# Two groups of query products instead of three, a stream shuffle for the rotary halves, and the rotary sums on POOL

## The reference

```python
q = _rms_norm(x @ w_qa, q_a_norm_w) @ w_qb          # 16 heads of 128 + 64
q_nope, q_rope = (q[..., :D_NOPE], q[..., D_NOPE:])
q_rope = q_rope * cos + rotate_half(q_rope) * sin   # (-x2, x1) on even and odd features
scores = einsum(q_full, k_full) * scale             # causal mask, softmax, times v
```

## Time and profile before

| | before |
|---|---|
| median of 3 runs | 1178.39 us (1176.42 to 1179.44) |
| the profiled execution | 1178.33 us, span 1176.4 us |
| mean granted TensorE clock | 0.985 |
| busy: PE, DVE, ACT, POOL | 1114.3, 818.9, 791.4, 699.2 us |
| three query matmuls, L1101 (32 pairs x 3 groups) | 96 groups |
| POOL `q_lo`, L904 | 64 times, 1341 ns mean |

### The profile page before, as it was taken

One profiled execution on the slowest core, in us unless ns is written; L12 is line 12 of the kernel. 1 busy time (PEld: TensorE's weight loads), 2 busy tenths in 40 slices (PEclk: granted clock), 3 DMA queues, 4 the chain that ended last, 5 costly groups with the idle time before them and its releaser, 6 DMA issues. The chain is left out here.

```text
span 1176.4 us, 27725 instructions
## 1 busy us (share of the span) xinstructions
PE 1114.3 (95%) x11356; PEld 930.9 (79%) x11356; DVE 818.9 (70%) x1825; ACT 791.4 (67%) x1104; POOL 699.2 (59%) x579
## 2 busy tenths in 40 slices
PE   5769999999999999999999999999999788999997
PEld 4747788888888888888888888888887687989886
DVE  3778767676767777676767778677676566675776
ACT  3737777877778787778778787877877543333232
POOL 1436776877777677877676776868777662130000
PEclk9889999999999999999999999999999989999999
DMA  9430100010002000100100020010000050000000
GB/s 241 111 116 17 32 20 9 12 48 20 20 2 65 2 20 26 41 20 2 54 12 20 1 65 15 6 48 20 19 2 2 15 166 1 1 19 1 19 18 18
DMA packets 58126, 39.60 MB, mean 34 GB/s; under 512 B 8113, under 2 KB 57329, under 8 KB 57841
## 3 DMA queue, kind: packets, MB, share of 16 engines
q1 hardware_dynamic: 56608, 33.81, 10.3%
q10 hardware_dynamic: 1392, 4.03, 1.3%
HBM read 33.37 MB, written 4.46 MB: 32 GB/s over the span
## 5 line engine op out<-in xcount | busy, mean ns | idle before, releaser
L912 POOL TENSOR_TENSOR pt_lo<-pt 128x1024 f16<-128x1024 f32 x192 | 370.4, 1940 | 182.1 <-ACT pt L969 181.8
L1031 DVE TENSOR_REDUCE gates<-bank 128x1 f32<-128x512 f32 x384 | 261.6, 689 | 147.8 <-PE bank L1113 144.9
L960 ACT ACTIVATE pair<-shift 128x1024 f32<-128x1024 f32 x256 | 263.5, 1029 | 12.5 <-ACT pt L973 0.7
L969 ACT ACTIVATE pt<-pair 128x1024 f32<-128x1024 f32 x192 | 196.0, 1021 | 110.0 <-PE pair L1141 109.3
L1156 PEld LDWEIGHTS bank<-values,pt 128*128 128x128 bf16 x2176 | 196.8, 98 | 80.4 <-issue 52.5
L1156 PE MATMUL bank<-values,pt 128*128 128x65 f16 x2176 | 235.2, 195 | 6.2 <-DVE lat L1057 5.5
L1158 PE MATMUL bank<-values,pt 128*128 128x64 f16 x2176 | 231.8, 192 | 0.0
L1160 PE MATMUL bank<-values,pt_lo 128*128 128x65 f16 x2176 | 230.8, 194 | 0.0
L918 POOL TENSOR_TENSOR pt_lo<-pt 128x512 f16<-128x512 f32 (+3 forms) x256 | 178.3, 723 | 46.4 <-ACT pt L973 46.3
L1158 PEld LDWEIGHTS bank<-values,pt 128*128 128x128 bf16 x2176 | 202.0, 98 | 0.0
L1160 PEld LDWEIGHTS bank<-values,pt_lo 128*128 128x128 f16 x2176 | 201.3, 97 | 0.0
(11 more groups left out here) (222 smaller groups left out, 2291.4 us busy)
## 6 DMA issues: line engine op xcount, KB each, us to landing
turn_by<-rope_cos_by_feature SPq DMA_DIRECT2D x64, 128.0 KB, 3.0
turn_by<-rope_sin_by_feature SPq DMA_DIRECT2D x64, 128.0 KB, 3.0
xs<-in_L_attn_x SPq DMA_DIRECT2D x4, 512.0 KB, 12.1
lat<-in_L_attn_w_o SPq DMA_DIRECT2D x1, 2048.0 KB, 9.5
xs_again<-in_L_attn_x SPq DMA_DIRECT2D x1, 2048.0 KB, 7.9
out<-xs_again SPq DMA_DIRECT2D x4, 512.0 KB, 2.8
lat<-in_L_attn_w_qb ACTq DMA_DIRECT2D x1, 1152.0 KB, 12.4
wq_parts<-wq_hi SPq DMA_DIRECT2D x1, 1152.0 KB, 7.3
```

Source lines behind the costliest of these rows:

```text
L912: pool.tensor_tensor(out=pt_lo[at][:, :, :].rearrange("p a n -> p (a n)"), in0=full, in1=cut(full), op=ALU.subtract).then_inc(low_ok, 1)
L960: act.activation(s_pair[u % 2][:, :, :], shift_of(item, 1).to_broadcast([P, 2, BW]), ACT.Copy).then_inc(seeded["a"], 1)
L969: act.activation(pt[at][:, :, :], s_pair[u % 2][:, :, :], ACT.Exp).then_inc(exp_done, 1)
L1031: dve.tensor_reduce(out=to, in_=of, axis=AXX, op=ALU.max).then_inc(work_seen["v"], 1)
```

## The change

The swapped copy of the rotary weights goes, and with it part 2. Part 0 now holds the rotary rows of both heads (head 1 on partitions 0 to 63, head 0 on 64 to 127), part 1 the absorbed rows of both. DVE multiplies part 0 once by the sine, already swapped in HBM, with the sign of each row as a scalar, and once by the cosine, into two SBUF buffers, and swaps neighbouring partitions of the sine product with a stream shuffle. The two 64x512 sums are made by DVE for the first two pairs and by POOL for the other thirty, in rounds 2 and 3 of a pair's preparation; ACT's `q_hi` follows a round behind each; POOL's two `q_lo` are in rounds 4 and 5. `query_plain` makes both absorbed copies in round 1 and still waits for the `q_lo` of the pair before. The buffers `by_sin` and `by_cos` are single. The `shift` ring goes from four slots to three, the buffers lie in another order, the stored query weights are a third smaller, and two small DMAs write the swapped sine at the start. DVE makes the sign column at the very start.

```diff
+POOL_SUMS = 2
+SUM_AT = {r + n: (p, n - 2) for p, r in enumerate(PREP_ROUND) for n in (2, 3)}
+LOW_AT = {r + n: (p, n - 4) for p, r in enumerate(PREP_ROUND) for n in (4, 5)}
 SHIFT_AT = {r: i for i, r in enumerate(SHIFT_ROUND)}
-PREP_AT = {r + n: (p, n) for p, r in enumerate(PREP_ROUND) for n in range(4)}
+PREP_AT = {r + n: (p, n) for p, r in enumerate(PREP_ROUND) for n in range(3)}
...
 for _r in ROUNDS:
     WORK_ORDER += [("max", c) for c in CHUNKS_AT[_r]]
     WORK_ORDER += [("shift", SHIFT_AT[_r])] if _r in SHIFT_AT else []
-    WORK_ORDER += [("q", *PREP_AT[_r])] if _r in PREP_AT and PREP_AT[_r][1] < 3 else []
+    WORK_ORDER += [("q", *PREP_AT[_r])] if _r in PREP_AT and PREP_AT[_r][1] < 2 else []
 WORK = {w: n for n, w in enumerate(WORK_ORDER)}
 
 
...
-        moves = []
-        for at, hd in ((KVL, 0), (P, 1)):
-            moves += [(at, 0, even[:, :, hd], 0), (at, 1, odd[:, :, hd], 0)]
-        for at, hd in ((2 * P, 1), (2 * P + DR, 0)):
-            moves += [(at, 0, odd[:, :, hd], 1), (at, 1, even[:, :, hd], 0)]
+        moves = [(at, e, (even, odd)[e][:, :, hd]) for at, hd in ((0, 1), (DR, 0)) for e in range(2)]
 
...
+            to, of = (w.rearrange("(i e) s -> e i s", e=2) for w in (k["sin_swapped"], k["sin_t"]))
+            for e in range(2):
+                sp.dma_start(to[e], of[1 - e]).then_inc(sines_out, 16)
...
+            for n, with_sign in enumerate((1.0, -1.0)):
+                dve.memset(picked[:, 0, :].rearrange("p (i e) -> p i e", e=2)[:, :, n], with_sign).then_inc(sign_ok, 1)
+            dve.wait_ge(sign_ok, 2)
+            dve.wait_ge(consts, 8)
+            dve.tensor_tensor(out=picked[:, 1, :], in0=picked[:, 0, :], in1=ident[:, :], op=ALU.mult).then_inc(sign_ok, 1)
+            dve.wait_ge(sign_ok, 3)
+            dve.tensor_reduce(out=sign[:, :], in_=picked[:, 1, :], axis=AXX, op=ALU.add).then_inc(sign_ok, 1)
...
-            rotary_low(4, 8)
...
-                        sp.wait_ge(work_done, WORK[("q", p - 1, 2)] + 1)
+                        sp.wait_ge(work_done, WORK[("q", p - 1, 1)] + 1)
...
-                pool.wait_ge(before["side_mm"], before["SIDE_AT"]["gate", 0] + 1)
-                pool.memset(ones_r[:, :].bitcast(F32), 1.0).then_inc(consts_ok, 1)
-
-                def query_low(p):
-                    for hd in range(2):
-                        pool.wait_ge(q_hi_ok, 2 * p + hd + 1)
-                        pool.tensor_tensor(out=q_lo[p % Q_SLOTS][:, hd, :], in0=qf[:, hd, :],
-                                           in1=q_hi[p % Q_SLOTS][:, hd, :].bitcast(F32), op=ALU.subtract).then_inc(q_lo_ok, 1)
+
+                def query_sum(p, hd, done):
+                    pool.wait_ge(q_lo_ok, 2 * p)
+                    pool.wait_ge(low_ok, done)
+                    pool.wait_ge(q_swapped, p + 1)
+                    pool.wait_ge(work_seen["v"], SEEN["v"][WORK[("q", p, 0)] + 1])
+                    pool.tensor_tensor(out=qf[ROT[hd], hd, :], in0=by_sin[ROT[hd], :], in1=by_cos[ROT[hd], :],
+                                       op=ALU.add).then_inc(q_sum, 1)
+                    pool.wait_ge(q_sum, 2 * p + hd + 1)
+
+                def query_low(p, hd):
+                    pool.wait_ge(q_hi_ok, 2 * p + hd + 1)
+                    pool.tensor_tensor(out=q_lo[p % Q_SLOTS][:, hd, :], in0=qf[:, hd, :],
+                                       in1=q_hi[p % Q_SLOTS][:, hd, :].bitcast(F32), op=ALU.subtract).then_inc(q_lo_ok, 1)
...
-                    p, part = PREP_AT.get(r, (0, 3))
-                    if part == 2:
-                        query_low(p)
+                    if r in SUM_AT and SUM_AT[r][0] >= POOL_SUMS:
+                        query_sum(*SUM_AT[r], OPS[min(r, NU - 1) + 1])
+                    if r in LOW_AT:
+                        query_low(*LOW_AT[r])
+                    if LOW_AT.get(r) == (0, 1):
+                        pool.wait_ge(before["wq_out"], 32)
+                        pool.memset(ones_r[:, :].bitcast(F32), 1.0).then_inc(consts_ok, 1)
 
             @block.scalar
             def _(act):
-                def query_plain(p, part):
-                    n = WORK[("q", p, part)]
-                    if part == 0 and p > 0:
+                def query_plain(p):
+                    n = WORK[("q", p, 1)]
+                    if p > 0:
                         act.wait_ge(q_lo_ok, 2 * p)
                     act.wait_ge(work_done, n + 1)
-                    act.activation(qf[PLAIN[part], part, :], work_of(n)[PLAIN[part], :], ACT.Copy).then_inc(work_seen["a"], 1)
-
-                def query_high(p):
+                    for hd in range(2):
+                        act.activation(qf[PLAIN[hd], hd, :], work_of(n)[PLAIN[hd], :], ACT.Copy).then_inc(work_seen["a"], 1)
+
+                def query_high(p, hd):
+                    wait_seen(act, WORK[("q", p, 1)])
                     if p >= Q_SLOTS:
                         act.wait_ge(s_done, 2 * FIRST_UNIT[2 * (p - Q_SLOTS) + 2])
-                    for hd in range(2):
-                        act.wait_ge(q_sum, 2 * p + hd + 1)
-                        act.activation(q_hi[p % Q_SLOTS][:, hd, :], qf[:, hd, :], ACT.Copy).then_inc(q_hi_ok, 1)
+                    act.wait_ge(q_sum, 2 * p + hd + 1)
+                    act.activation(q_hi[p % Q_SLOTS][:, hd, :], qf[:, hd, :], ACT.Copy).then_inc(q_hi_ok, 1)
...
-                    if part < 2:
-                        query_plain(p, part)
-                    if part == 2:
-                        query_high(p)
+                    if part == 1:
+                        query_plain(p)
+                    if r - 1 in SUM_AT:
+                        query_high(*SUM_AT[r - 1])
 
             @block.vector
             def _(dve):
-                def query_turn(p, part):
-                    n = WORK[("q", p, part)]
-                    if part == 0:
-                        if p > 0:
-                            dve.wait_ge(q_lo_ok, 2 * p)
-                        dve.wait_ge(turn_in[p % 2], 64 * (p // 2 + 1))
+                def query_turn(p):
+                    n = WORK[("q", p, 0)]
+                    dve.wait_ge(turn_in[p % 2], 64 * (p // 2 + 1))
+                    if p == 0:
+                        dve.wait_ge(before["sign_ok"], 4)
+                    else:
+                        dve.wait_ge(q_sum, 2 * p)
                     dve.wait_ge(work_done, n + 1)
-                    if part < 2:
-                        rot = ROT[part]
-                        dve.tensor_tensor(out=qf[rot, part, :], in0=work_of(n)[rot, :], in1=turn_by[rot, p % 2, 0, :],
-                                          op=ALU.mult).then_inc(work_seen["v"], 1)
-                    else:
-                        dve.tensor_tensor(out=work_of(n)[:, :], in0=work_of(n)[:, :], in1=turn_by[:, p % 2, 1, :],
-                                          op=ALU.mult).then_inc(q_turned, 1)
-                        query_sum(p)
+                    dve.scalar_tensor_tensor(out=by_sin[:, :], in0=work_of(n)[:, :], scalar=sign[:, :], in1=turn_by[:, p % 2, 1, :],
+                                             op0=ALU.mult, op1=ALU.mult).then_inc(work_seen["v"], 1)
+                    dve.tensor_tensor(out=by_cos[:, :], in0=work_of(n)[:, :], in1=turn_by[:, p % 2, 0, :],
+                                      op=ALU.mult).then_inc(work_seen["v"], 1)
+
+                def query_swap(p):
+                    dve.wait_ge(work_seen["v"], SEEN["v"][WORK[("q", p, 0)] + 1])
+                    dve.stream_shuffle(by_sin[:, :], by_sin[:, :], [i ^ 1 for i in range(32)]).then_inc(q_swapped, 1)
 
                 def query_sum(p):
-                    for part in range(2):
-                        wait_seen(dve, WORK[("q", p, part)])
-                    dve.wait_ge(q_turned, p + 1)
-                    by_sin = work_of(WORK[("q", p, 2)])
+                    if p > 0:
+                        dve.wait_ge(q_lo_ok, 2 * p)
+                    dve.wait_ge(work_seen["v"], SEEN["v"][WORK[("q", p, 0)] + 1])
+                    dve.wait_ge(q_swapped, p + 1)
                     for hd in range(2):
-                        dve.tensor_tensor(out=qf[ROT[hd], hd, :], in0=by_sin[ROT[hd], :], in1=qf[ROT[hd], hd, :],
+                        dve.tensor_tensor(out=qf[ROT[hd], hd, :], in0=by_sin[ROT[hd], :], in1=by_cos[ROT[hd], :],
                                           op=ALU.add).then_inc(q_sum, 1)
...
-                    p, part = PREP_AT.get(r, (0, 4))
-                    if part < 3:
-                        query_turn(p, part)
+                    p, part = PREP_AT.get(r, (0, 3))
+                    if part == 2 and p < POOL_SUMS:
+                        query_sum(p)
+                    if part == 0:
+                        query_turn(p)
+                    if part == 1:
+                        query_swap(p)
...
```

More of the change, by code:

```diff
@@ L89, in chunks_at @@
     return CHUNKS_AT[r][n:] if half else CHUNKS_AT[r][:n]
+POOL_SUMS = 2
+SUM_AT = {r + n: (p, n - 2) for p, r in enumerate(PREP_ROUND) for n in (2, 3)}
```

(40 more changed lines are left out.)

50 lines of the change are left out of this document (24 added, 26 removed).

## The result

The changed kernel takes 1200.86 us (median of 4 runs, 1200.02 to 1202.66) against 1177.41 for the kernel before: a ratio of 1.020, 95% interval 1.019 to 1.022. It is 2% slower. The forecast was 1187 (1162 to 1197): slower was right, but the loss is 23.5 us and not 9, outside the range. The profiled execution took 1202.66, its span is 1200.4.

A forecast was written before the change was run, and what follows sets the result against it. The prediction took PE (TensorE) to bound the attention stage. Six cycles cost +17.6 us, the eight pairs outside gain 5.7 and the start 3.4: net +8.5 on 1178.33, so 1187 us, range 1162 to 1197.

The forecast's parts named there:

- The dropped group: On PE, the third group of three query matmuls goes for 32 pairs: 0.72 us each, 22.9 us off.
- The sum on POOL: A 64x512 sum takes POOL 1.27 us, 1.5 us with its self-waits; two per pair for 30 pairs.
- The shuffle: DVE's one shuffle per pair, taken as 0.69 us, at most 1.4; no profile row showed one.
- The four-apart place: Where pairs are four rounds apart (six places), ACT waits for q_lo and PE for the seed (3.0 us): 4.8 us lost.
- Rivals 1 and 2: First: PE gets the whole saving, 1152 us, chance 0.08. Second: a 64-partition POOL sum is short, 1166 us, chance 0.09.
- rival 3: Only one of two waits costs, ACT's seed wait or POOL's lateness: -9 us, 1170 us, chance 0.13.
- rival 5: Gain and loss cancel, slack off by half a microsecond at each point: 1175 to 1182 us, chance 0.09.
- a cycle: +2.9: Four pairs gain 2.9 us on PE and lose 4.8 + 1.0 to waits; six cycles cost +17.6 us.
- the eight pairs outside of them gain 5.7: The eight pairs outside the six cycles gain 5.7 us from dropped PE groups, with no loss priced.
- the eight-apart place: Where pairs are eight rounds apart (one per weight pair), POOL's last q_lo is 1.0 us late for PE.
- the start: DVE's products and shuffle of pair 1 run before its wait for q_lo, and pair 2 is shorter: 3.4 us gained.
- rival 4: POOL is blocked more by DVE, a sum taking 1.9 us instead of 1.5: 1195 to 1203 us, chance 0.06.

The follow-up runs named there:

- e5: Changed kernel, all sums on DVE, cosine product written back to its PSUM bank, shuffle and sums first in DVE's next round, q_lo in rounds 2 and 3: 1242.25 us.
- e6: As e5, but with the shuffle one round earlier, behind the evacuation: 1242.15 us.
- e3: Changed kernel with all sums on DVE, plus 60 additions on POOL that nothing reads or waits for: 1191.87 us.
- the second trace: The changed kernel run again unchanged, for another trace: 1199.67 us.
- the first trace: The changed kernel's original profiled execution: 1202.66 us.
- e10: e9 with pairs prepared at least six rounds apart (from pair 3 on): 1154.15 us.
- e7: The kernel before the change, making only the first matmul of the third group of three: 1167.74 us.
- e1: Changed kernel with all 64 rotary sums on DVE, none on POOL: 1165.05 us.
- e9: e1 with one sum in each of two DVE rounds (2 and 3), sums and shuffle behind the evacuation: 1158.41 us.

## Why the prediction was half right

**Right, by its own steps.** The dropped group takes 0.7 us off at each of pairs 3 to 27 (the unit after it starts 0.69 to 0.71 earlier, against the kernel before, than the unit before it, in every trace with two groups but those of e5 and e6). The sum on POOL: 1.27 predicted, 1.287 measured; two low parts with a sum between them start 3.39 apart (255.94, 259.33), so that a sum occupies 3.39 - 1.89 = 1.5, as priced. The shuffle: 0.69 predicted, 0.79 measured; no sum on POOL waits for it. The four-apart place: the `q_lo` that ACT waits for was worked out to end 12.1 us after POOL's start of unit 60; measured 12.0 (255.94 to 267.94). Unit 66 starts 3.0 us late, as forecast, and the place costs 4.7 us against 4.8. Rivals 1 and 2 fell with the rows of `q_lo` and L907; rival 3, with both waits found; rival 5, with the time.

**Right with some luck.** Of the 3.0 us, the first 1.8 (unit 64) come by a path that the prediction does not have: DVE's products wait for POOL's second sum, because `by_sin` and `by_cos` are single. It took them to be free and priced no wait. The total is right because ACT's chain ends no earlier than this one; e3 shows 2.6 us without it.

**Wrong: the terms "a cycle: +2.9" and "the eight pairs outside of them gain 5.7".** I searched for places with too little slack by the distance between pairs, and took every other place as free.

- A cycle loses 3.8. The missing 0.9 is mostly the eight-apart place at 1.3 (1.0 forecast) and 0.6 at the third kind of place (sixteen apart), priced at nothing. Six cycles (units 38 to 270) lose 22.9 us in the second trace in place of 17.6: 5.3 us.
- Outside the cycles and at the start I had -9.1. The second trace has 21.3 - 22.9 = -1.6. Of the 3.4 us of the start 2.9 do arrive, but the pairs outside, forecast to gain 5.7, lose about 1. Pair 3 costs 0.9 (unit 15), pair 4 1.0 (units 30 and 31), and after unit 280 four places cost 0.5 to 1.1 each. That makes 7.5 us.
- 1187 + 5.3 + 7.5 = 1199.8 against the second trace's 1199.67. The second term is what the first leaves of the measured difference, so that the sum closes says nothing by itself.
- In the first trace the start gained only 0.3. It has 7 us more at the lower clock there, which fits, but no run shows that this is the reason.

The time is in the range of rival 4 (1195 to 1203), and in part for its reason, POOL disturbed by DVE, but not at the sums, where it had put the cost.

**What the price of those places is made of.** In part it is the work as I priced it, and in part something I had no term for: POOL's load falls on DVE as well, and DVE's on POOL. DVE's `spread` reads `ident` and `nmx`, both in SBUF. At the eight-apart place and at the sixteen-apart one, kernel after:

```profile
230.81 2.15 DVE L1058 TENSOR_TENSOR spread<-ident,nmx 128x512 fp32r<-128x512 f32 x1
```

```profile
232.36 1.73 POOL L913 TENSOR_TENSOR q_lo<-qf,q_hi 128x512 fp32r<-128x512 f32 x1
```

```profile
318.57 1.74 DVE L1058 TENSOR_TENSOR spread<-ident,nmx 128x512 fp32r<-128x512 f32 x1
```

```profile
319.71 1.73 POOL L913 TENSOR_TENSOR q_lo<-qf,q_hi 128x512 fp32r<-128x512 f32 x1
```

Each `spread` (0.69 alone) is held up by POOL's instruction before, and each `q_lo` (1.28 alone) by the `spread`. By tile, before, after, and e10:

```profile
L1041 DVE TENSOR_TENSOR spread<-ident,nmx x64: 691/693/2380, 79.7 to 924.4; 128x512 fp32r<-128x512 f32 x64
```

```profile
L1058 DVE TENSOR_TENSOR spread<-ident,nmx x64: 691/1042/2395, 77.6 to 949.0; 128x512 fp32r<-128x512 f32 x64
```

```profile
L1057 DVE TENSOR_TENSOR spread<-ident,nmx x64: 691/693/2384, 78.3 to 902.0; 128x512 fp32r<-128x512 f32 x64
```

It was over 1 us in 7 of 64 before, in 33 after and in 20 in e10, 55.9 us in all before and 78.2 after. POOL's `q_lo` was over 1.5 us in 7 of 64 before and 14 after, 1 in e10, each time beside a `spread`. Part of this goes by timing alone: e7, with no new work on POOL, has 21 long `spread`. The fair comparison is e1, the changed kernel without POOL's sums: 12 of 64 and 59.5 us, and two long `q_lo`. So the sums on POOL lengthen `spread` by 19 us in all; e3's idle additions do it too (32 of 64, 68.3 us).

At both places the first `q_lo` takes 1.73 us, 0.45 more than priced; the eight-apart place cost 0.34 over the forecast and the sixteen-apart one 0.6. That these waits are the rest of the loss is argued from these rows, not shown by a run of its own. Rival 4 named blocking, but as DVE blocking a sum (L907 was over 1.5 in 6 of 60, at most 1.57), and gave it 0.06.

I read in the earlier trace rows that `q_lo` goes up to 1.74 and gave it no term. Its cause was readable before: which DVE instructions have both inputs in SBUF, and how often the changed POOL would meet them.

## What to carry to other kernels

A matmul taken from a saturated PE is worth its slot only if every queue beside it has the slack, and that slack is to be looked up at every kind of place, not at the tightest two. Before work goes from DVE to POOL, or an operand from PSUM to SBUF, list the DVE instructions with two SBUF inputs: here two of them, `spread` and in e1 the sums, and POOL's instructions held each other up, so load on POOL was load on DVE too. Count single buffers as waits: a buffer that one engine fills and a slower one empties ties the first to the second. And when a stage is in step, spreading one-off work over rounds (e9) and over the schedule (e10) gained some 11 us on top of e1, where moving it to the engine with the most idle time cost 36.

## What the runs showed of the hardware

- POOL: 64x512 and 128x512 f32 take the same (1.287 and 1.281 us); an addition whose two inputs are the same 120-column row, read four times over, took 0.985 for 64x480, 18% less than length alone gives.
- DVE: a stream shuffle of 128x512 f32 takes 0.71 to 0.81 us, and 0.01 for its mask.
- DVE and POOL exclude each other when DVE reads two SBUF operands: the same 64x512 sum takes 0.69 us alone and up to 2.38 behind a 1.89 us POOL instruction; with one operand in PSUM it is 0.68 to 0.69 in 64 of 64, 36 of them beside a busy POOL (e5).
- TensorE's clock: between 60 and 100 us the same program spent about 17 us at 0.50 in one execution and 10 in another, and unit 0 began 2.6 us later in the first. In e5, where PE idles some 1.8 us in nearly every pair, the granted clock is 0.97 on the mean from 100 to 900 us, and 1.00 in e1.
